# A layer kernel: x of most groups loaded already transposed and normalised by GpSimd, the k maxima folded into ScalarE's exp, and VectorE's steps on two PSUM banks merged

## The chip, the cores and the metric

The kernel runs on one core of a Trainium2 chip. The metric is device time in microseconds (us) of one execution. TensorE (PE), VectorE (DVE), ScalarE (ACT), GpSimd (POOL) and SyncE (SP, which only issues DMAs here) each work through a program of their own, in order, and meet at semaphores.

## The reference, cut to what matters

```
x: (128, 64, 256) f32;  8 heads of 32 channels;  cond: (128, 512)
xn = layernorm(x) * ln_w + ln_b
q  = softmax over the 32 channels of a head ( xn @ Wq + bq )
k  = softmax over the 64 tokens of a batch  ( xn @ Wk + bk + (1 - mask) * -1e6 )
v  = (xn @ Wv + bv) * mask
att = k^T v per batch and head;  y = q @ att
scale, shift = split( silu(cond) @ W_emb + b_emb )
h  = layernorm(y) * ln2_w + ln2_b;  h = h * (1 + scale) + shift
out = x + silu(h) @ W_out + b_out
```

## The kernel before

The 8192 rows of x are cut into 16 groups of 512 tokens (8 batches each, T = 4 tiles of 128 tokens). A group passes through three stages, and the order is written out by hand for each engine: in turn i, `body(i, ...)` does the front stage F of group i (transposed x, k, q, v), the middle stage B of group i-1 (attention and y) and the back stage O of group i-2 (second layer norm, silu, output product). Turns 3 to 14 are a loop of two turns, the others are unrolled, and a tail finishes the last groups. The helper `steps` calls `body`; N means that a next group exists.

**TensorE** in a turn: 8 transposes of the normalised x (L1059, into the banks bt), 8 transposes of exp(k) of the group before (L961), the k product (12 matmuls, `k_high` and `k_low`: every fp32 operand is split in a high and a low part, so each product is three), 8 transposes of y (L973), 8 of exp(q) (L982), 128 small attention matmuls, the q and v product of tiles 0 and 1, 128 small y matmuls, the q and v product of tiles 2 and 3, and the output product of the group two back (24 matmuls). All matmuls have the line of the helper, L905.

**ScalarE** copies the transposed x out of PSUM (this makes the high part xt_hi, L533), copies exp(k), exp(q) (L498, L515), does exp of k and q (L509, L505), tanh (L521, into the SBUF tile th), the v copies (L489), the high part of h (L526), the mask offset (L482), and normalises the four x tiles of the next group, row by row, with a scale and a bias per partition (L558).

**GpSimd** subtracts the k maxima from k (L356, two 128x512 steps), adds the shift to z (L271), takes the layer norm roots of x and of y (chains of four and of two tiny steps, each waiting for the one before, L402 to L408 and L420, L422), the low part of h (L367), normalises y (L425, four tiles) and adds b_out to x (`x_biased`, L375, one 128x1024 step).

**VectorE**: low part of x (L804, PSUM bank minus xt_hi, one step per bank), masked k and its maxima (L815, L819), z = y^T times the modulation (L735), statistics of x (L632, L636), the scaled attention kv (L747, L751), h = (tanh + 1) * z (L759, from th and z_s), q maxima and q minus them (L722, L727, one step per tile), y by its sums (L770, L775), statistics of y (L784 to L792) and the residual (L798, one step per bank).

**SyncE** loads x and the mask rows and stores the output; all transfers of a turn go through its one queue in the order of its program.

PSUM has 8 banks: be (two), bt (two) and the two pairs bk and bv. The four banks be and bt are also the tile by of the y product. A bank is written again only after its readers have counted up the semaphores that the writer waits for.

Of the kernel before, what the change touches and what calls it, by code (L numbers as in the profile page):

```python
# [20 lines left out]
def build_layer(nc, x, cond_t, columns_in, b_qvk, mask_rows, wq, wk, wv, w_emb, w_out, b_out, out):  # L21
# [23 lines left out]
    with ctx:  # L45
# [36 lines left out]
        xr = sb("xr", [P, 4, T])  # L82
        xhat = sb("xhat", [P, 2, T, D])
# [17 lines left out]
        th = sb("th", [P, C, GT])  # L101
        h_s = sb("h_s", [P, C, GT])
# [6 lines left out]
        h_t = xhat[:, 0, :, :].rearrange("p (c t) d -> p c (t d)", c=C)  # L109
# [12 lines left out]
        def bank(name):  # L122
            return ctx.enter_context(nc.psum_tensor(name, [P, 512], fp32))
# [3 lines left out]
        bk_ = [bank("bk0"), bank("bk1")]  # L127
        bv_ = [bank("bv0"), bank("bv1")]
# [14 lines left out]
        x_in = [sem("x_in0"), sem("x_in1")]  # L143
        x_first = [sem("x_first0"), sem("x_first1")]
# [80 lines left out]
        def steps(eng, body, tail, after_first=None):  # L225

            def at(i):
                body(i, i % 2, i + 1 < G, 0 <= i < G, 0 <= i - 1 < G, 0 <= i - 2 < G)
# [6 lines left out]
            with eng.Fori(1, G // 2 - 1) as turn:  # L235
                body(2 * turn + 1, 1, True, True, True, True)
                body(2 * turn + 2, 0, True, True, True, True)
            at(G - 1)
            tail()
# [4 lines left out]

        def first(i):

            return isinstance(i, int) and i == 0
# [25 lines left out]

        x_h = x.rearrange("(g t p) d -> g p t d", t=T, p=P)
# [12 lines left out]
        def _(sp):  # L287
# [15 lines left out]
            for n in range(2):  # L303
                sp.dma_start(w_e[n][:, :, :], w_emb[n * 2 * P:(n + 1) * 2 * P, :]
                             .rearrange("(c p) n -> p c n", p=P)).then_inc(we_in, 16)
            sp.dma_start(w_o, w_out.rearrange("(c p) n -> p c n", p=P)).then_inc(wo_in, 16)
            load_off(1, 1)
            sp.dma_start(bo_all[:, :], b_out[None, :].broadcast_to([P, D])).then_inc(bo_in, 16)

# [5 lines left out]
            def body(i, par, N, F, B, O):  # L315

                if N and not (isinstance(i, int) and i < 1):
                    wait(sp, xstat_d, 4 * i)
                    load_x(i + 1, 1 - par)
                    wait(sp, kadd_d, 2 * i)  # L320
                    load_off(i + 1, 1 - par)
                if O and not (isinstance(i, int) and i < 3):
                    store(i - 3)

# [18 lines left out]
        def _(pool):  # L343
# [6 lines left out]
            pool.memset(v_s[:, :, :, :, DH:AW], 1.0).then_inc(pool_init, 1)  # L350

            def k_shifted(g, parity, c):

                wait(pool, kmax_d, 2 * g + c + 1)
                kk = k_t[:, parity, c, :].rearrange("p (b s) -> p b s", s=SEQ)
# [13 lines left out]

            def x_biased(g):  # L370
                if isinstance(g, int) and g == 0:
                    pool.wait_ge(bo_in, 16)
                wait(pool, xhat_d, 4 * g + 4)
# [4 lines left out]
            def body(i, par, N, F, B, O):  # L378
                if F and not first(i):
                    k_shifted(i, par, 0)  # L380
                if O:
                    if isinstance(i, int) and i == 2:
                        pool.wait_ge(mod_ready, C)
                    shifts(i - 2)
                if last_turn(i):
                    k_shifted(i, par, 1)
                    x_biased(i)
                if N and isinstance(i, int) and i < 0:
                    pool.wait_ge(pool_init, 1)
                    pool.wait_ge(xmv_d, T)  # L390
                    nc.gpsimd.tensor_scalar(xr[:, 0, :], xmv[:, :, 1], 1.0, EPS, ALU.mult, ALU.add).then_inc(xr_d, 1)
                    pool.wait_ge(xr_d, 1)
                    nc.gpsimd.tensor_tensor(xr[:, 1, :], xr[:, 0, :], neg_half[:, :], ALU.pow).then_inc(xr_d, 1)
                    pool.wait_ge(xr_d, 4)
                    for t in (2, 3):
                        nc.gpsimd.tensor_scalar(xhat[:, 0, t, :], x_all[:, 0, t * D:t * D + D], xr[:, 1, t:t + 1],
                                                xr[:, 3, t:t + 1], ALU.mult, ALU.add).then_inc(xhat_d, 1)
                elif N:
                    g = i + 1
                    wait(pool, xhat_d, 4 * g)  # L400
                    wait_apart(pool, xmv_d, 4 * g + 4)
                    nc.gpsimd.tensor_scalar(xr[:, 0, :], xmv[:, :, 1], 1.0, EPS, ALU.mult, ALU.add).then_inc(xr_d, 1)  # L402
                    wait(pool, xr_d, 4 * g + 1)
                    nc.gpsimd.tensor_tensor(xr[:, 1, :], xr[:, 0, :], neg_half[:, :], ALU.pow).then_inc(xr_d, 1)
                    wait(pool, xr_d, 4 * g + 2)
                    nc.gpsimd.tensor_tensor(xr[:, 2, :], xmv[:, :, 0], xr[:, 1, :], ALU.mult).then_inc(xr_d, 1)
                    wait_apart(pool, xr_d, 4 * g + 3)
                    nc.gpsimd.tensor_scalar(xr[:, 3, :], xr[:, 2, :], -1.0, 1.0, ALU.mult, ALU.add).then_inc(xr_d, 1)  # L408
                if O:
                    for c in range(C):  # L410
                        h_low(i - 2, c)
                if first(i):
                    k_shifted(i, par, 0)
                if F and not last_turn(i):
                    k_shifted(i, par, 1)
                if B:
                    g = i - 1
                    wait(pool, yhat_d, 4 * g)
                    wait(pool, yve_d, 2 * g + 2)
                    nc.gpsimd.tensor_tensor(yr[:, 1, :], yr[:, 0, :], neg_half[:, :], ALU.pow).then_inc(yr_d, 1)  # L420
                    wait(pool, yr_d, 2 * g + 1)
                    nc.gpsimd.tensor_tensor(yr[:, 3, :], yr[:, 2, :], yr[:, 1, :], ALU.mult).then_inc(yr_d, 1)  # L422
                    wait_apart(pool, yr_d, 2 * g + 2)
# [3 lines left out]
                if F and not last_turn(i):  # L427
                    x_biased(i)

# [22 lines left out]
        def _(act):  # L452
# [19 lines left out]
            def emb_copied():  # L472

                act.wait_ge(emb_done, 1)
                for j in range(2 * C):
                    nc.scalar.activation(emb[:, j, :], be[1][:, j * BATCH:(j + 1) * BATCH], ACT.Identity,
                                         scale=0.5, bias=b_e[:, j:j + 1]).then_inc(emb_out, 1)

# [15 lines left out]
            def exp_k_copied(g):  # L494
                for e in range(2):
                    wait(act, ekt_d, 2 * g + e + 1)
# [673 lines left out]
```

## Time and profile before

| | us |
|---|---|
| median of 3 runs | 321.76 |
| lowest and highest run | 320.66, 323.11 |
| the profiled execution, whole | 320.57 |
| the profiled execution, span from first to last instruction | 318.8 |
| TensorE busy in the span | 305.2 |
| VectorE busy in the span | 276.6 |
| GpSimd busy in the span | 229.2 |
| ScalarE busy in the span | 192.7 |

The durations in the rows come from the profiled execution: 1.8 us of its time lie outside of the span, and the median of the runs is 1.2 us above it. Busy time counts the union of an engine's instructions. TensorE's instructions overlap, so a group's busy time divided by its count says what one costs the engine; the mean duration of one is longer.

### The profile page before, as it was taken

To read this page: it belongs to the slowest core of one execution; us is meant where nothing else is said; L and a number is where in the kernel's file an instruction comes from. 1 tells how busy PE (TensorE), PEld (TensorE's weight loads), DVE (VectorE), ACT (ScalarE), POOL (GpSimd) and SP (SyncE) were. 2 spreads that over 40 slices of the span, in tenths; PEclk is the share of its full clock that TensorE was granted. 3 is DMA by queue.
4 is the path that set the end of the run, shared out by engine and by line. 5 is a ranking of instruction groups with operands and counts; after the bars stand their busy time and mean duration, and the time that the engine had idled before them with its cause. 6 is when DMAs were issued, how large, how long until landed. Compare 5 with 4: busy or idle time off the path is not lost.

```text
span 318.8 us, 14540 instructions
## 1 busy us (share of the span) xinstructions
PE 305.2 (96%) x5650; PEld 261.3 (82%) x5650; DVE 276.6 (87%) x749; ACT 192.7 (60%) x378; POOL 229.2 (72%) x276
## 2 busy tenths in 40 slices
PE   6999989999999999999999999999999999998964
PEld 5587767889888898889888898889888898987854
DVE  3876989799898989899898989899898989889784
ACT  1556557656575757757575757657575748655350
POOL 2181479868777978878787888878787888886550
PEclk9999999999999999999999999999999999999978
DMA  6940301230504041130505041230505010100023
GB/s 218 348 117 1 103 3 37 64 105 4 167 3 148 16 132 33 62 102 0 164 0 153 11 132 33 67 98 0 164 0 153 11 66 0 67 4 4 2 69 132
DMA packets 21706, 23.84 MB, mean 75 GB/s; under 512 B 1073, under 2 KB 19121, under 8 KB 21682
## 3 DMA queue, kind: packets, MB, share of 16 engines
q1 hardware_dynamic: 20736, 22.94, 23.4%
q10 hardware_dynamic: 946, 0.57, 0.6%
q8 instruction: 17, 0.28, 0.4%
q14 instruction: 7, 0.06, 0.1%
HBM read 15.12 MB, written 8.39 MB: 74 GB/s over the span
## 4 chain that ended last, share of the span: by engine, by line
PE 81%; DVE 12%; issue 2%; DMA 2%; POOL 1%; ACT 1%; SPq 0%; DVEq 0%; POOLq 0%
PE bk L905 27%; PE bv L905 26%; PE by L905 13%; PE by L982 4%; PE bv L973 4%; PE by L961 4%; PE by L1059 4%; DMA q_t<-in_wv 2%; DVE ystat L784 1%; DVE h_s L759 1%; DVE y_s L775 1%; DVE xt_lo L804 1%; DVE xstat L632 1%; DVE q_s L727 1%; DVE qmax L722 1%
## 5 line engine op out<-in xcount | busy, mean ns | idle before, releaser
L509 ACT ACTIVATE k_t<-k_t 128x512 f32<-128x512 f32 x32 | 20.0, 626 | 42.9 <-POOL k_t L356 42.9
L356 POOL TENSOR_TENSOR k_t<-k_t,kmax 128x512 f32<-128x512 f32 x32 | 33.9, 1060 | 16.1 <-DVE kmax L819 16.1
L367 POOL TENSOR_TENSOR h_lo<-h_s,h_hi 128x512 fp32r<-128x512 f32 x30 | 39.1, 1325 | 2.5 <-ACT h_hi L526 1.9
L271 POOL TENSOR_TENSOR z_s<-z_s,mod_shift 128x512 f32<-128x512 f32 x30 | 30.7, 1045 | 14.2 <-DVE z_s L735 14.2
L375 POOL TENSOR_TENSOR x_all<-x_all,bo_all 128x1024 f32 (+1 forms) x16 | 38.9, 2433 | 0.0
L558 ACT ACTIVATE xhat<-x_all,xr 128x256 f32 (+1 forms) x62 | 32.2, 592 | 5.1 <-DVE xr L643 3.7
L425 POOL TENSOR_SCALAR y_s<-y_s,yr 128x256 f32<-128x256 f32 x60 | 32.8, 561 | 2.5 <-POOL yr L422 2.2
L815 DVE SCALAR_TENSOR_TENSOR k_t<-off,bk 128x512 f32<-128x512 f32 x32 | 21.8, 682 | 14.5 <-PE bk L905 14.5
L533 ACT ACTIVATE xt_hi<-by 128x512 fp32r<-128x512 f32 x32 | 17.4, 597 | 25.2 <-PE by L1059 25.2
L905 PE MATMUL bv<-w_o_hi,h_hi 128*128 128x256 f32 x120 | 32.2, 287 | 0.0
L905 PE MATMUL bv<-w_o_lo,h_hi 128*128 128x256 f32 x120 | 32.0, 288 | 0.0
L905 PEld LDWEIGHTS by<-kv,q_t 32*64 32x64 f32 x2048 | 22.4, 130 | 6.4 <-issue 5.3
L420 POOL TENSOR_TENSOR yr<-yr,neg_half 128x4 f32<-128x4 f32 x15 | 15.2, 1013 | 17.1 <-DVE yr L792 17.1
L905 PE MATMUL bk<-xt_hi,w_k_hi 128*128 128x512 f32 x64 | 26.6, 416 | 0.7 <-ACT xt_hi L533 0.7
L521 ACT ACTIVATE th<-z_s 128x512 f32<-128x512 f32 x30 | 18.9, 633 | 13.0 <-POOL z_s L271 13.0
L905 PE MATMUL bk<-xt_hi,w_k_lo 128*128 128x512 f32 x64 | 25.3, 395 | 0.0
L905 PE MATMUL by<-kv,q_t 32*64 32x33 f32 x2048 | 24.5, 226 | 0.4 <-issue 0.2
L905 PE MATMUL bv<-w_o_hi,h_lo 128*128 128x256 f32 x120 | 24.2, 283 | 0.0
L819 DVE TENSOR_REDUCE kmax<-k_t 128x8 f32<-128x512 f32 x32 | 22.0, 686 | 2.2
L905 PEld LDWEIGHTS bv<-w_o_hi,h_hi 128*128 128x128 f32 x120 | 23.2, 193 | 0.6
L905 PEld LDWEIGHTS bv<-w_o_lo,h_hi 128*128 128x128 f32 x120 | 23.1, 193 | 0.6
L804 DVE TENSOR_TENSOR xt_lo<-by,xt_hi 128x512 fp32r<-128x512 f32 x32 | 20.6, 685 | 3.2 <-ACT xt_hi L533 3.2
(128 smaller groups left out, 864.3 us busy)
## 6 DMA issues: line engine op xcount, KB each, us to landing
x_all<-in_x SPq DMA_DIRECT2D x15, 512.0 KB, 4.4
out<-x_all SPq DMA_DIRECT2D x15, 512.0 KB, 3.2
off<-in_mask_rows SPq DMA_DIRECT2D x16, 256.0 KB, 3.3
x_all<-in_x SPq DMA_DIRECT2D x2, 256.0 KB, 3.4
z_s<-in_w_emb SPq DMA_DIRECT2D x1, 512.0 KB, 9.2
h_s<-in_w_emb SPq DMA_DIRECT2D x1, 512.0 KB, 11.1
out<-x_all SPq DMA_DIRECT2D x2, 256.0 KB, 2.6
y_s<-in_wk ACTq DMA_DIRECT2D x1, 256.0 KB, 4.1
```

Of the source, the lines that this page charges most:

```text
L271: return eng.tensor_tensor(z, z, mod_shift[:, c, span(g, GB)].unsqueeze(2).broadcast_to([P, GB, SEQ]), ALU.add)
L356: nc.gpsimd.tensor_tensor(kk, kk, kmax[:, c, :].unsqueeze(2).broadcast_to([P, GB, SEQ]), ALU.subtract).then_inc(ksub_d, 1)
L367: nc.gpsimd.tensor_tensor(h_lo[:, c, :], h_s[:, c, :], h_hi[:, c, :].bitcast(fp32), ALU.subtract).then_inc(hlo_d, 1)
L375: nc.gpsimd.tensor_tensor(xg, xg, bo_all[:, :].unsqueeze(1).broadcast_to([P, T, D]), ALU.add).then_inc(xb_d, 1)
L425: nc.gpsimd.tensor_scalar(y_s[:, t, :], y_s[:, t, :], yr[:, 1, t:t + 1], yr[:, 3, t:t + 1], ALU.mult, ALU.add).then_inc(yhat_d, 1)
L509: nc.scalar.activation(k_t[:, parity, c, :], k_t[:, parity, c, :], ACT.Exp).then_inc(kexp_d, 1)
L521: nc.scalar.activation(th[:, c, :], z_s[:, c, :], ACT.Tanh, scale=0.5).then_inc(th_d, 1)
L558: nc.scalar.activation(xhat[:, 1 - par, t, :], group_of(x_all, g)[:, :, t * D:t * D + D].rearrange("p g n -> p (g n)"), ACT.Identity, scal ...
L804: nc.vector.tensor_tensor(xt_lo[:, c, :], bt[c][:, :], xt_hi[:, c, :].bitcast(fp32), ALU.subtract).then_inc(lo_d, 1)
L815: nc.vector.scalar_tensor_tensor(k_t[:, par, c, :], off[:, par, :], -1000000.0, bk_[c][:, :], ALU.mult, ALU.add).then_inc(kadd_d, 1)
L819: nc.vector.tensor_reduce(out=kmax[:, c, :], in_=k_t[:, par, c, :].rearrange("p (b s) -> p b s", s=SEQ), axis=AX.X, op=ALU.max).then_inc(k ...
L905: return nc.tensor.matmul(dst, lhsT, rhs, start=start, stop=stop)
```

## The change

The host gives a second input, x_t, which is x transposed. From group 2 on the transposes of x on TensorE are gone. Instead, SyncE loads the transposed raw x of the group (512 KB) into xt_raw. Its normalisation is now per column, so the layer norm's two numbers per token have to lie along the free axis, in every partition: GpSimd makes them per token as before (`x_rstd`), VectorE turns the 128x32 tile by blocks (`x_rows`), SyncE writes the rows to DRAM with four small DMAs (`rows_stored`) and reads them back broadcast to all partitions (`rows_loaded`, 4 KB per partition), and GpSimd multiplies and adds in place (`x_scaled`, two 128x512 steps per half of the channels). ScalarE makes the high part from xt_raw at the end of the turn before (`x_high`), VectorE the low part of both halves in one step (`x_low`).

From group 1 on `k_shifted` is gone. VectorE writes the negated masked k and takes its minimum; ScalarE's exp takes scale -1 and the minimum as bias. That works for one batch at a time, so the two exp steps of a group become sixteen steps of 128x64.

The four steps that normalise y move from GpSimd to ScalarE, at the start of the next turn (`y_hat_all`), except for the last groups. ScalarE's four steps on x are gone from group 2 on.

tanh is written to the PSUM banks bt instead of the SBUF tile th, once exp(q) is copied out of them. The y product waits for the h steps that read it there (wait on h_d).

VectorE's q maxima, q subtraction, k-v reciprocals, scaled y, low part of x and residual are done in one step for two banks each. x is loaded and its statistics are taken three groups ahead instead of one. The first turns and a few orders change with it.

The loop now covers turns 3 to 12. The core of the diff:

```diff
@@ SyncE
+            def load_xt(g, parity):
+                sp.dma_start(xt_raw[:, parity, :, :], xt_h[:, :, span(g, GT)]).then_inc(xt_in[parity], 16)
+            def rows_stored(g, parity):
+                wait(sp, xrow_d, g - 1)
+                wait(sp, rows_in, 16 * g - 48)
+                for n in range(4):
+                    sp.dma_start(rows_dram[parity].rearrange("k (t p) -> (k t) p", p=P)[:, 32 * n:32 * n + 32],
+                                 xr_rows[32 * n:32 * n + 2 * T, :]).then_inc(rows_out, 16)
+            def rows_loaded(g, parity):
+                wait(sp, rows_out, 64 * g - 64)
+                wait(sp, xs_d, 2 * g - 4)
+                sp.dma_start(rows[:, :, :].rearrange("p k n -> p (k n)").unsqueeze(1),
+                             rows_dram[parity:parity + 1].rearrange("o k n -> o (k n)").unsqueeze(0)
+                             .broadcast_to([P, 1, 2 * GT])).then_inc(rows_in, 16)
+            def body(i, par, N, F, B, O, S):
...
+                if S:
+                    wait(sp, xstat_d, 4 * i + 5)
+                    load_x(i + 3, 1 - par)
+                if N and not first(i):
                     wait(sp, kadd_d, 2 * i)
                     load_off(i + 1, 1 - par)
+                if not (isinstance(i, int) and i + 2 >= G):
+                    rows_stored(i + 2, par)
                 if O and not (isinstance(i, int) and i < 3):
                     store(i - 3)
+                if not (isinstance(i, int) and i + 2 >= G):
...
+                        load_xt(i + 2, par)
+                    rows_loaded(i + 2, par)
@@ GpSimd
-            def k_shifted(g, parity, c):
...
+            def x_scaled(g, parity, c):
+                if c == 0:
+                    wait(pool, rows_in, 16 * g - 16)
+                    wait(pool, xt_in[parity], 8 * (g - parity))
+                xc = xt_raw[:, parity, c, :]
+                nc.gpsimd.tensor_tensor(xc, xc, rows[:, 0, :], ALU.mult).then_inc(xm_d, 1)
+                wait(pool, xm_d, 2 * g + c - 3)
+                nc.gpsimd.tensor_tensor(xc, xc, rows[:, 1, :], ALU.add).then_inc(xs_d, 1)
...
+                for c in range(C):
+                    if N and c == 0 and not first(i):
+                        x_scaled(i + 1, 1 - par, c)
+                    if O:
                         h_low(i - 2, c)
+                    if N and c == 1 and not first(i):
+                        x_scaled(i + 1, 1 - par, c)
                 if B:
+                    y_scale(i - 1)
...
+                if S and not first(i):
+                    x_rstd(i + 3)
+                if not last_turn(i):
+                    x_biased(i)
@@ ScalarE
+            def x_high(g, parity, c):
+                wait(act, xs_d, 2 * g + c - 3)
+                wait(act, qv_d, 4 * g)
+                nc.scalar.activation(xt_hi[:, c, :], xt_raw[:, parity, c, :], ACT.Copy).then_inc(hi_d, 1)
             def k_exp(g, parity, c):
-                wait(act, ksub_d, 2 * g + c + 1)
-                nc.scalar.activation(k_t[:, parity, c, :], k_t[:, parity, c, :], ACT.Exp).then_inc(kexp_d, 1)
+                wait(act, kmax_d, 2 * g + c + 1)
+                for n in range(GB):
+                    kk = k_t[:, parity, c, n * SEQ:n * SEQ + SEQ]
+                    last = nc.scalar.activation(kk, kk, ACT.Exp, scale=-1.0, bias=kmax[:, c, n:n + 1])
+                last.then_inc(kexp_d, 1)
 (order of a turn: y_hat_all(i-2); exp_k_copied 0; q_exp(i-1, half 1); exp_k_copied 1; k_exp(i, 0);
  q_copied; z_tanh into bt; v_tile 0; h_high 0; v_tile 1; h_high 1; k_exp(i, 1); v_tile 2; v_tile 3;
  mask_offset; x_high(i+1, 0 and 1); q_exp(i, half 0))
@@ VectorE
+            def x_low(i, full):
+                wait(dve, hi_d, 2 * i + 2)
+                nc.vector.tensor_tensor(xt_lo[:, :, :], full, xt_hi[:, :, :].bitcast(fp32),
+                                        ALU.subtract).then_inc(lo_d, 2)
+            def x_rows(g):
+                wait(dve, xr_d, 4 * g + 4)
+                wait(dve, rows_out, 64 * g - 128)
+                nc.vector.transpose(xr_rows[:, :], xr[:, :, :].rearrange("p a t -> p (a t)")).then_inc(xrow_d, 1)
 (order of a turn: k_masked 0; k_max 0; k_masked 1; z_scaled(i-2); k_max 1; kv_scaled(i-1); h_product(i-2) 0, 1;
  x_stats(i+3); q_max 0; y_sums(i-1); q_shifted 0; y_scaled_all(i-1); y_stats(i-1); q_max 1; x_rows(i+2);
  q_shifted 1; x_low(i+1, xt_raw); residual_all(i-2))
@@ TensorE
-                if F:
-                    for c in range(C):
...
-                            last = nc.tensor.transpose(bt[c][:, t * P:t * P + P], xhat[:, par, t, c * P:c * P + P],
...
                 if B:
+                    wait(pe, h_d, 2 * i - 2)
                     y_product(i - 1)
```

## Rows read from the trace of the kernel before

**Rows 1.** The page: busy times, and the granted clock in 40 slices

```profile
PE 305.2 (96%) x5650; PEld 261.3 (82%) x5650; DVE 276.6 (87%) x749; ACT 192.7 (60%) x378; POOL 229.2 (72%) x276
...
PEclk9999999999999999999999999999999999999978
```

**Rows 2.** Windows: turns 3 to 14, then turn 15

```profile
60.92:275.53 214.61, 214.61 (x4179) 186.29 (x4178) 195.24 (x541) 140.43 (x277) 173.65 (x204) 1.00 0.23 70
275.53:290.95 15.42, 14.47 (x318) 11.72 (x317) 13.52 (x23) 9.19 (x18) 13.51 (x11) 1.00 0.11 37
```

**Rows 3.** Chain that ended last, k products of turns 9, 10

```profile
169.37 2.93 PE bk L905 x12
...
187.28 2.83 PE bk L905 x12
```

**Rows 4.** The same chain in turn 2 (start, us, what)

```profile
43.05 1.29 DVE xt_lo L804 x2
```

**Rows 5.** The same chain in turn 15 and the tail

```profile
285.04 2.85 DVE h_s L759
...
290.81 1.31 DVE ystat L784 x4
...
294.29 2.17 POOL y_s L425 x4
```

**Rows 6.** Groups of instructions by line, of all engines

```profile
L1059 PE MATMUL by<-ident,xhat 128*128 128x128 f32 x128 | 16.6, 273 | 0.0
...
L367 POOL TENSOR_TENSOR h_lo<-h_s,h_hi 128x512 fp32r<-128x512 f32 x30 | 39.1, 1325 | 2.5 <-ACT h_hi L526 1.9
L356 POOL TENSOR_TENSOR k_t<-k_t,kmax 128x512 f32<-128x512 f32 x32 | 33.9, 1060 | 16.1 <-DVE kmax L819 16.1
L425 POOL TENSOR_SCALAR y_s<-y_s,yr 128x256 f32<-128x256 f32 x60 | 32.8, 561 | 2.5 <-POOL yr L422 2.2
...
L422 POOL TENSOR_TENSOR yr<-yr 128x4 f32<-128x4 f32 x15 | 3.0, 200 | 1.2
...
L509 ACT ACTIVATE k_t<-k_t 128x512 f32<-128x512 f32 x32 | 20.0, 626 | 42.9 <-POOL k_t L356 42.9
...
L476 ACT ACTIVATE emb<-by,small 128x128 f32<-128x128 f32 x4 | 1.1, 369 | 0.2 <-PE by L905 0.2
...
L770 DVE RECIPROCAL rq<-by 128x32 f32<-128x32 f32 x16 | 5.5, 346 | 0.9 <-PE by L905 0.9
```

**Rows 7.** Timeline of turn 9, TensorE

```profile
167.46 1.04 PE L1059 MATMUL by<-ident,xhat 128*128 128x128 f32 x8
...
168.33 1.04 PE L961 MATMUL by<-ident,k_t 128*128 128x128 f32 x8
```

**Rows 8.** Timeline of turn 9, VectorE

```profile
171.11 0.69 DVE L815 SCALAR_TENSOR_TENSOR k_t<-off,bk 128x512 f32<-128x512 f32 x1 [1.00 <-PE bk L905]
...
173.83 1.28 DVE L735 TENSOR_TENSOR z_s<-bv,mod_scale 128x512 f32<-128x512 f32 x2
...
177.58 1.28 DVE L759 SCALAR_TENSOR_TENSOR h_s<-th,z_s 128x512 f32<-128x512 f32 x2
178.78 0.75 DVE L722 TENSOR_REDUCE qmax<-bv 128x8 f32<-128x256 f32 x2
```

**Rows 9.** Timeline of turn 9, GpSimd

```profile
177.16 1.02 POOL L404 TENSOR_TENSOR xr<-xr,neg_half 128x4 f32<-128x4 f32 x1
178.25 0.67 POOL L406 TENSOR_TENSOR xr<-xmv,xr 128x4 f32<-128x4 f32 x1
```

**Rows 10.** Timeline of turn 15, VectorE, then GpSimd

```profile
283.78 4.12 DVE L759 SCALAR_TENSOR_TENSOR h_s<-th,z_s 128x512 f32<-128x512 f32 x2
...
284.53 2.82 POOL L375 TENSOR_TENSOR x_all<-x_all,bo_all 128x1024 f32<-128x1024 f32 x1
```

**Rows 11.** The page: DMA queues and issues

```profile
q1 hardware_dynamic: 20736, 22.94, 23.4%
...
x_all<-in_x SPq DMA_DIRECT2D x15, 512.0 KB, 4.4
```

More of the change, by code:

```diff
@@ L233, in steps @@
                 at(i)
[L235 to L238, printed above, removed]
+            with eng.Fori(1, G // 2 - 2) as turn:
+                body(2 * turn + 1, 1, True, True, True, True, True)
+                body(2 * turn + 2, 0, True, True, True, True, True)
+            for i in (G - 3, G - 2, G - 1):
+                at(i)
             tail()
@@ L272, in shift, with first @@
                                      ALU.add)
+        def first(i):
+            return isinstance(i, int) and i == 0
+        xt_h = x_t.rearrange("(c p) n -> p c n", p=P)
         x_h = x.rearrange("(g t p) d -> g p t d", t=T, p=P)
@@ L384, in body @@
                     shifts(i - 2)
+                if first(i):
+                    k_shifted(0)
+                    k_shifted(1)
+                    x_rstd(2)
                 if last_turn(i):
-                    k_shifted(i, par, 1)
                     x_biased(i)
[L388 to L408, printed above, removed]
@@ new lines, in x_high_turned, with x_hat_one @@
+            def x_high_turned(g):
+                for c in range(C):
+                    act.wait_ge(xt_d, 2 * g + c + 1)
+                    wait(act, qv_d, 4 * g)
+                    nc.scalar.activation(xt_hi[:, c, :], bt[c][:, :], ACT.Copy).then_inc(hi_d, 1)
+            def x_hat_one():
+                act.wait_ge(xr_d, 8)
+                act.wait_ge(xt_d, 2)
+                for t in range(T):
+                    nc.scalar.activation(xhat[:, t, :], x_all[:, 1, t * D:t * D + D], ACT.Identity,
+                                         scale=xr[:, 0, t:t + 1], bias=xr[:, 1, t:t + 1]).then_inc(xhat_d, 1)
@@ new lines, in emb_copied, with k_exp_first, exp_k_copied @@
+            def emb_copied():
+                act.wait_ge(emb_done, 1)
+                for j in range(2 * C):
+                    nc.scalar.activation(emb[:, j, :], be[1][:, j * BATCH:(j + 1) * BATCH], ACT.Identity,
+                                         scale=0.5, bias=b_e[:, j:j + 1]).then_inc(emb_out, 1)
+            def k_exp_first(c):
+                act.wait_ge(ksub_d, c + 1)
+                nc.scalar.activation(k_t[:, 0, c, :], k_t[:, 0, c, :], ACT.Exp).then_inc(kexp_d, 1)
+            def exp_k_copied(g, e):
+                wait(act, ekt_d, 2 * g + e + 1)
+                wait(act, att_d, g)
+                nc.scalar.activation(e_k[:, 2 * e:2 * e + 2, :].rearrange("p t d -> p (t d)"), be[e][:, :],
+                                     ACT.Copy).then_inc(ek_d, 1)
@@ new lines, in body @@
+                v_tile(i, par, 1)
+                if O:
+                    h_high(i - 2, 1)
+                if first(i):
+                    x_hat_one()
+                else:
+                    k_exp(i, par, 1)
+                v_tile(i, par, 2)
+                if first(i):
+                    k_exp_first(1)
+                    emb_copied()
+                v_tile(i, par, 3)
+                if N:
+                    mask_offset(i + 1, 1 - par)
+                    if first(i):
+                        x_high_turned(1)
+                    else:
+                        for c in range(C):
+                            x_high(i + 1, 1 - par, c)
@@ L1033, in out_product, with x_transposed @@
                           ).then_inc(o_d, 1)
+            def x_transposed(g):
+                pe.wait_ge(xhat_d, 4 * g + 4)
+                for c in range(C):
+                    for t in range(T):
+                        last = nc.tensor.transpose(bt[c][:, t * P:t * P + P], xhat[:, t, c * P:c * P + P], ident[:, :])
+                    last.then_inc(xt_d, 1)
             def k_high(i, c):
```

373 lines of the change are left out of this document (203 added, 170 removed).

## The prediction

> **What bounds the kernel now.** The page comes first: TensorE is busy for 305 of 318.8 us at a granted clock of 9 tenths or more until the very end, so the clock plays no part, and VectorE follows with 87% [rows 1]. A share over the span hides where each engine is full, so the windows come next. Turns 3 to 14 take 214.61 us, 17.88 each, and TensorE is busy in all of it; per turn VectorE works 16.27 us, GpSimd 14.47 and ScalarE 11.70 [rows 2]. In these turns the path is TensorE's own list of work. The chain of waits says the same: its k product takes 2.93 and 2.83 us in two turns following one another [rows 3], so there is a stall of 0.1 us for the low part of x in one of two turns, and nothing more. Outside of the loop it is otherwise. In turn 2 the chain runs through VectorE and reaches the k product through the low part of x [rows 4]. In turn 15 TensorE is busy for 14.47 of 15.42 us [rows 2], and the chain runs through an h step of 2.85 us on VectorE and four y steps on GpSimd [rows 5].
>
> **The change on TensorE.** It loses eight transposes of x per group. They start at 167.46, the next eight at 168.33 [rows 7]: 0.87 us on the path, not the 1.04 that the row shows as busy nor 8 times 273 ns. The group row gives the same order, 16.6 us for 128, 1.04 per eight, the overlap with the neighbour included [rows 6]. With the 0.05 us of mean stall a turn's floor is 17.88 - 0.87 - 0.05 = 16.96 us. For turns 3 to 14 that would be 12 x 0.92 = 11.0 us. Whether it is reached depends on whether the others fit in 17 us and keep their order.
>
> **VectorE**, per turn. Merged steps save an instruction's fixed part: the pair of 128x256 steps takes 0.75 us, one step of 128x512 takes 0.69 [rows 8], so a merge is worth 0.06. The q maxima and the q subtraction are two merges each, the reciprocals, scaled y, low part of x and residual one each: 8 x 0.06 = 0.5 us. `x_rows` adds a 128x32 step: its nearest rows are the 0.35 us of another 128x32 step [rows 6] and nothing at all; I take 0.2. Sum: 16.27 - 0.5 + 0.2 = 16.0 us (15.8 to 16.1). It fits into 17, with the 1.00 us in which it waits for k now [rows 8], a wait that stays, since the residual and the first k bank hang on two moments of TensorE's turn 2.5 us apart.
>
> **ScalarE.** Four x steps leave and four y steps of the same kind come: nothing. Two exp steps of 0.63 [rows 6] become sixteen of 128x64 with a bias per partition. No row shows that shape. The nearest is the emb copy, 128x128 with such a bias: 4 in 1.1 us of which the last takes 0.37, so 0.25 from start to start [rows 6]. Half the columns can't cost more; from below I take 0.2. Sum: 11.70 - 1.25 + 16 x 0.24 = 14.3 us (13.7 to 14.6), well below 17. The Trainium skill (ScalarE: Activation LUTs, What ACT_TABLE_LOAD costs) gives an ACTIVATE with a pointer bias as 280 ns plus 0.833 ns per column and an overlap of 93 ns back to back; an estimate from it is 240 ns for 64 columns. By it the sum would be the same; for the shape with 128 columns it gives 387 ns where the row has 369, so trace and page agree.
>
> **GpSimd** loses k minus maxima (2 x 1.06) and the four y steps (32.8 us for 60, so 2.19 [rows 6]), and gets four steps of 128x512 on two full operands. Nearest rows: 1.06 us with a broadcast operand, 1.325 for h_lo with two full ones [rows 6]. `rows` is a full operand, so I take 1.25. Sum: 14.47 - 2.12 - 2.19 + 5.0 = 15.2 us (14.4 to 15.5), to which waits between dependent steps add some 0.3. It fits, but the order matters, so I lay out a turn, each step with the time it has in turn 9 now and the new ones with the prices above. Zero is the start of the transposes of exp(k) (168.33 in turn 9); TensorE's work follows in its old order.
>
> - k masked at 2.7 as before (171.11 is 2.78 [rows 8]); z now ahead of the second maximum, at 4.8 instead of 5.5 (173.83 [rows 8]).
> - GpSimd: shifts 5.5 to 7.6, first x half to 10.2, low parts of h to 12.8, second x half to 15.3, y root to 16.8, x root to 18.9, `x_biased` to 21.3. That is 4.3 in the next turn, where the shifts are due at 5.5. TensorE needs the low parts of h at about 14.5: 1.7 to spare.
> - ScalarE: exp of k until 6.2, q copied 7.2, tanh to 8.3, x high at 15.4 and 16.0 after mask offset, half of exp(q) to 17.1, y steps to 2.3 in the next turn; TensorE transposes y at 3.7.
> - VectorE: h until 9.1, statistics of x to 10.8, y statistics to 15.3, `x_rows` at 16.0, x low 16.7 to 17.9, residual to 19.0, which is 2.0 of the next turn, ahead of k at 2.7. The low part is needed at 1.8 and is there at 0.9.
> - New wait on TensorE: the y product waits for h, since tanh lies in its banks. It is due at 9.6, h is done at 9.1: 0.5 to spare. Behind it in the queue stand two q and v tiles and the output product, and everything waits.
>
> Every margin is positive, the thinnest are 0.5 and 1.2 us. I take a turn of 17.05 us, 0.09 above the floor, for small waits like those of now. Turns 3 to 14: 12 x 0.83 = 10.0 us.
>
> **The new transfers.** `x_rows` at 16.0, four small DMAs issued one by one in 1.6 us, landing, then the broadcast read of 512 KB, issued behind a store and the load of the transposed x. A load of 512 KB takes 4.4 us from issue to landing [rows 11]; the packets of q1 take 23.4% of 16 engines for 22.94 MB, so 512 KB occupy them for 1.7 us. Written at 17.6, landed at about 19.8, read issued at 20.1, landed between 23.5 (nothing ahead) and 26.0 (two transfers of 1.7 us ahead, less what has passed of them). In the next turn this is 6.5 to 9.0. GpSimd wants it at 7.6 and can take it until 9.4 before the low parts of h come late to the output product. So it costs nothing in this sum, by up to 2 us of cover. Traffic rises by about 1 MB a turn, to 40% of the engines.
>
> **Start.** The first turns exchange work: statistics of x come earlier, `weights_o` moves from turn 1 to turn 0, where VectorE waited for v. VectorE's low part of x for group 2 ends at 44.33 now [rows 4]; adding the merged and moved steps I find the same within 0.5 us. From there TensorE has no x transposes at the head of turn 3: 0.9 saved (0 to 1.5).
>
> **Turn 15.** Now the two h steps of this turn take 4.12 us instead of 1.28, while GpSimd runs its 128x1024 step, which takes 2.82 [rows 10]. Both inputs of h, th and z_s, lie in SBUF. In the changed kernel tanh lies in PSUM. The small steps show the other side of it: in turn 9 a 128x4 step takes 0.67 us with the h steps at work (177.58 to 178.86), while its kind takes 0.20 [rows 6, 8, 9]. So the collision goes. The 2.85 us step is on the chain, which goes on through the y statistics to the four y steps of GpSimd [rows 5]; without the wait it takes the 0.68 of its kind, 2.17 less. Not all of that comes back, since y also waits for TensorE's y product. In my layout the statistics of y begin at 13.6 in the turn; now they begin at 290.81 - 275.53 = 15.3 [rows 2, 5]. That is 1.7 us, and with a little lost in the tail I take 1.6 for turn 15 and tail together (0.8 to 2.2).
>
> **Sum.** 0.9 + 10.0 + 1.6 = 12.5 us. The profiled execution took 320.57 in all, so 308.1; the median lies 1.2 above it, so 309.3. I say 309.
>
> **Rivals.**
> Small waits each turn, at 20%: exp pieces at 0.3 us would put tanh and h 0.5 us later and use up the margin before the y product; GpSimd's steps at the upper end do the same to the low parts of h. Against it: every row is below that. At 17.4 us a turn: 12 x 0.48 + 2.5 = 8.3, 313.5 us.
>
> No gain, at 11%: the rows come late. Each us beyond 9.4 holds GpSimd, and behind it in its queue the low parts of h and TensorE's output product. The path from one `x_rows` through the output product spans two turns, so half of it counts per turn. To cancel the 0.83 us of a turn it takes a landing 1.7 us beyond 9.4, 12 us after `x_rows`. Then only start and end remain: 319.3 us. For it speaks that four transfers, a store and a load share one queue; against it the 4.4 us of a load as it is.
>
> Slower, at 11%: the two-input steps move to a worse place. `x_low` takes xt_raw and xt_hi, both in SBUF, where it took a PSUM bank before. It runs near the end of the turn, where GpSimd soon starts its 2.4 us `x_biased`. In my layout it starts at 16.7 and GpSimd's step at 18.9, and only tiny steps meet it. If x high comes over 2.2 us late, `x_low` meets `x_biased` and waits as h did in turn 15, 2.85 - 0.68 = 2.17 us, with TensorE's k product behind it: 17.05 + 2.17 = 19.22 us a turn, 12 x 1.34 - 2.5 = 13.6 us slower, 335 us. The Trainium skill (SBUF — State Buffer, SBUF: two separate sides) states that a VectorE operation with two SBUF inputs and a GpSimd operation exclude each other for a whole instruction, whichever starts first; the 4.12 us pair agrees. By that rule the change also gives relief in each turn, since h leaves it and `x_low` enters.
>
> **Chances and range.** The forecast has 58%, the three rivals 20, 11 and 11. The lower end is the floor, 16.96 a turn, with the best start and end: 11.0 + 1.5 + 2.2 = 14.7, or 307, less the 1.2 us by which runs differ: 305.5. The upper end takes in small waits and stops short of no gain: 318. A difference within 1% is about what this kernel's runs can't tell from none. Faster by over 1%: the forecast and the first rival, 0.78; within: 0.11; slower: 0.11.
>
> **What would show it.** Turn length from one L961 group to the next at 17.0 to 17.1; no idle time of TensorE before the y product put down to h, none before k put down to x_lo; exp pieces 0.2 to 0.26 us apart; GpSimd's x steps at 1.25; the broadcast read landed before the shifts of z end; h pair at 1.3 in turn 15. Wrong it would be if GpSimd stood waiting for the rows for over 2 us a turn, if its x steps took over 1.6, or if `x_low` showed durations over 2 us.

## The result and the profile after

The changed kernel takes 342.34 us in the median of 4 runs (335.77 to 344.56), the kernel before 321.95 (320.66 to 323.11). The ratio is 1.050, with an interval of 1.043 to 1.058: the change makes the kernel 5% slower, where 309 us was forecast. Medians and ranges take in all executions; the ratios, here and below, leave out those that fell in a slower state of the chip. The profiled execution took 335.77 us, with a span of 333.9.

The page of the changed kernel, busy times and granted clock, to be held against [rows 1]:

```profile
PE 302.2 (90%) x5538; PEld 253.7 (76%) x5538; DVE 274.2 (82%) x639; ACT 236.1 (71%) x588; POOL 245.0 (73%) x247
...
PEclk9799978999979999999999999999999999999789
```

TensorE is idle for 31.7 us of the span, against 13.6 before, and its clock, which was at its upper level nearly throughout, has dips. The windows of turns 3 to 14, of turn 15, of the tail, and of two short stretches in turns 2 and 4 (columns: PE, PEld, DVE, ACT, POOL busy, clock, DMA share, GB/s; [rows 2] has the same of before):

```profile
67.97:289.33 221.36, 208.92 (x4083) 176.90 (x4081) 189.09 (x439) 175.37 (x444) 187.52 (x175) 0.99 0.40 124
289.33:303.38 14.05, 14.05 (x319) 11.79 (x317) 11.79 (x20) 11.96 (x32) 10.50 (x7) 1.00 0.12 40
303.38:333.90 30.52, 21.74 (x385) 20.31 (x383) 19.60 (x48) 10.37 (x18) 11.09 (x15) 0.87 0.16 53
48.00:54.00 6.00, 4.89 (x15) 3.89 (x16) 3.60 (x7) 4.04 (x9) 5.59 (x7) 0.58 0.46 141
91.30:98.60 7.30, 5.21 (x78) 3.95 (x76) 4.13 (x14) 2.73 (x6) 4.45 (x5) 0.77 0.53 166
```

Turns 3 to 14 take 18.45 us each, TensorE works 17.41 of them, and no engine is full: VectorE works 15.76 us a turn, GpSimd 15.63, ScalarE 14.61. The forecast had 16.0, 15.2 (to 15.5) and 14.3, so the work was sized nearly right. What was added is waiting. Against the forecast of 60.0, 204.6 and 43.3 - 1.6 = 41.7 us for the three stretches, the start takes 68.0 us (8 over), turns 3 to 14 take 221.4 (17 over), turn 15 and the tail 44.6 (3 over).

The chain of waits names the way in the middle of the kernel. Around turn 8 it leaves TensorE altogether (start, us, what):

```profile
146.27 6.45 DMA x_all<-in_x
152.94 0.44 DVE xstat L741
...
160.16 0.21 DVE xr_rows L751
160.49 0.30 SPq L315
...
162.11 0.42 SPq L348
162.79 0.40 SPq L308
163.43 0.69 SPq L322
164.42 6.71 DMA x_all<-in_x
171.37 0.44 DVE xstat L741
```

This is a ring. The statistics of x begin at 152.94. VectorE reaches `x_rows` 7.2 us later. SyncE's queue has waited for it: four row writes (L315), a store (L348), the transposed x (L308), the read of the rows (L322), and only behind them the load of x, at 164.42, 4.3 us after `x_rows`. It lands 6.7 us later, and the next statistics, which have waited for it, begin at 171.37. Once round is 18.4 us, the length of this turn (18.46). The waits (us in total, times, longest) show VectorE waiting for x, GpSimd waiting for the rows themselves, and where the delay reaches TensorE: the k product waits until the late q subtraction has read its bank.

```profile
POOL xt_raw L424 <- DMA rows<-rows_dram: 15.6, 12, 2.6
...
DVE xstat L741 <- DMA x_all<-in_x: 11.7, 9, 1.7
...
PE bk L1058 <- DVE q_s L845: 9.3, 10, 1.7
```

A load of 512 KB of x takes 6.4 us to land now, against 4.4 [rows 11]; the broadcast read of the rows takes 5.8. From the page:

```profile
x_all<-in_x SPq DMA_DIRECT2D x15, 512.0 KB, 6.4
...
rows<-rows_dram SPq DMA_DIRECT2D x14, 512.0 KB, 5.8
```

The start has another cause. VectorE's modulation in turn 1, five steps of 0.28 to 0.35 us in the kernel before, from the timeline of after:

```profile
36.19 0.99 DVE L818 TENSOR_SCALAR emb<-emb 128x256 f32<-128x256 f32 x1
37.22 1.26 DVE L820 TENSOR_SCALAR mod_scale<-emb,small 128x128 f32<-128x128 f32 x1
38.40 1.37 DVE L822 SCALAR_TENSOR_TENSOR mod_shift<-emb,small 128x128 f32<-128x128 f32 x1
39.70 1.37 DVE L820 TENSOR_SCALAR mod_scale<-emb,small 128x128 f32<-128x128 f32 x1
40.99 0.34 DVE L822 SCALAR_TENSOR_TENSOR mod_shift<-emb,small 128x128 f32<-128x128 f32 x1
```

Three of the five are as long as one of GpSimd's steps on x, the first takes 0.99, and the last, when GpSimd is done, its normal 0.34. GpSimd's four steps on x run in just this time:

```profile
35.73 1.30 POOL L424 TENSOR_TENSOR xt_raw<-xt_raw,rows 128x512 f32<-128x512 f32 x1 [1.20 <-DMA rows<-rows_dram]
37.11 1.29 POOL L426 TENSOR_TENSOR xt_raw<-xt_raw,rows 128x512 f32<-128x512 f32 x1
38.36 1.26 POOL L424 TENSOR_TENSOR xt_raw<-xt_raw,rows 128x512 f32<-128x512 f32 x1
39.70 1.28 POOL L426 TENSOR_TENSOR xt_raw<-xt_raw,rows 128x512 f32<-128x512 f32 x1
```

The modulation takes from 36.19 to 41.33, 5.1 us instead of 1.3. TensorE idles behind it, and its k product of turn 2 takes 4.82 us, in the stretch whose mean granted clock is 0.58; the k product of turn 1 takes 3.26 in the same profile (29.81 to 33.08). And in turn 4 the chain has a gap that no engine explains:

```profile
90.45 0.89 PE by L1058 x56
91.34 2.09 issue
93.42 0.55 PE by L1058 x30
93.97 4.53 PE bv L1058 x12
```

TensorE waits 2.1 us for nothing that the profile shows, in the middle of its attention matmuls, and then does in 4.53 us what takes 2.99 at full clock; the mean granted clock of the stretch is 0.77.

### The profile page after: what moved, and what is told of

Its sections match the earlier page's. It is cut to its first block, busy times and chain, and to the rows that moved or that the text cites. A ratio compares the mean times of both kernels' runs of the same rounds, so it can differ in the third digit from the quotient of the medians.

```text
span 333.9 us, 14365 instructions
## 1 busy us (share of the span) xinstructions
PE 302.2 (90%) x5538; PEld 253.7 (76%) x5538; DVE 274.2 (82%) x639; ACT 236.1 (71%) x588; POOL 245.0 (73%) x247
## 4 chain that ended last, share of the span: by engine, by line
PE 35%; DVE 20%; DMA 18%; issue 13%; SPq 8%; ACT 2%; POOL 2%; DVEq 1%; POOLq 1%
DMA x_all<-in_x 15%; PE bv L1058 12%; PE bk L1058 11%; PE by L1058 6%; DVE y_s L918 4%; SPq L315 3%; DVE ystat L933 3%; DVE xstat L741 3%; DVE q_s L845 2%; PE by L1135 2%; DMA q_t<-in_wv 2%; SPq L322 2%; PE bv L1126 2%; DVE ymv L936 1%; DVE rq L913 1%
## 5 line engine op out<-in xcount | busy, mean ns | idle before, releaser
L615 ACT ACTIVATE k_t<-k_t,kmax 128x64 f32<-128x64 f32 x240 | 60.5, 336 | 6.2 <-DVE kmax L863 6.1
L424 POOL TENSOR_TENSOR xt_raw<-xt_raw,rows 128x512 f32<-128x512 f32 x28 | 36.2, 1293 | 15.6 <-DMA rows<-rows_dram 15.6
L455 POOL TENSOR_TENSOR x_all<-x_all,bo_all 128x1024 f32 (+1 forms) x16 | 40.1, 2508 | 0.2
L426 POOL TENSOR_TENSOR xt_raw<-xt_raw,rows 128x512 f32<-128x512 f32 x28 | 36.1, 1288 | 2.2
L569 ACT ACTIVATE y_s<-y_s,yr 128x256 f32<-128x256 f32 x56 | 29.1, 590 | 10.8 <-POOL yr L447 10.8
L1058 PE MATMUL bk<-xt_hi,w_k_hi 128*128 128x512 f32 x64 | 27.7, 433 | 9.6 <-DVE q_s L845 9.3
L741 DVE BATCH_NORM_STATS2 xstat<-x_all 128x6 f32 (+1 forms) x64 | 22.4, 413 | 11.7 <-DMA x_all<-in_x 11.7
L1058 PE MATMUL bv<-w_o_lo,h_hi 128*128 128x256 f32 x120 | 31.7, 285 | 0.0
L554 ACT ACTIVATE v_s<-bk,small 128x256 f32<-128x256 f32 x32 | 15.2, 476 | 20.5 <-PE bk L1058 19.3
L433 POOL TENSOR_SCALAR xr<-xmv 128x4 f32<-128x4 f32 x15 | 14.9, 993 | 15.8 <-DVE xmv L745 12.3
L1058 PEld LDWEIGHTS bv<-w_o_hi,h_hi 128*128 128x128 f32 x120 | 23.3, 194 | 3.7 <-DVE q_s L845 3.3
L1058 PE MATMUL by<-v_s,e_k 64*32 64x33 f32 x2048 | 21.1, 201 | 4.7 <-issue 3.0
L1058 PEld LDWEIGHTS by<-v_s,e_k 64*32 64x32 f32 x2048 | 19.1, 105 | 7.7 <-issue 5.7
L554 ACT ACTIVATE v_s<-bv,small 128x256 f32<-128x256 f32 x32 | 15.1, 475 | 13.5 <-PE bv L1058 13.5
```

Of the source, the lines that this page charges most:

```text
L424: nc.gpsimd.tensor_tensor(xc, xc, rows[:, 0, :], ALU.mult).then_inc(xm_d, 1)
L426: nc.gpsimd.tensor_tensor(xc, xc, rows[:, 1, :], ALU.add).then_inc(xs_d, 1)
L433: nc.gpsimd.tensor_scalar(xr[:, 2, :], xmv[:, :, 1], 1.0, EPS, ALU.mult, ALU.add).then_inc(xr_d, 1)
L455: nc.gpsimd.tensor_tensor(xg, xg, bo_all[:, :].unsqueeze(1).broadcast_to([P, T, D]), ALU.add).then_inc(xb_d, 1)
L554: nc.scalar.activation(v_s[:, par, t, :, 0:DH], bqv[t][:, D:2 * D].rearrange("p (h d) -> p h d", d=DH), ACT.Copy, scale=mask_c[:, i * T + ...
L569: nc.scalar.activation(y_s[:, t, :], y_s[:, t, :], ACT.Identity, scale=yr[:, 1, t:t + 1], bias=yr[:, 3, t:t + 1]).then_inc(yhat_d, 1)
```

## The experiments

**Load of x a turn earlier.** x_all has room for all groups, so the load can leave before the row writes.

```diff
-                if S:
-                    wait(sp, xstat_d, 4 * i + 5)
-                    load_x(i + 3, 1 - par)
+                if first(i):
+                    wait(sp, xstat_d, 5)
+                    load_x(3, 1)
...
+                if not (isinstance(i, int) and i + 4 >= G):
+                    wait(sp, xstat_d, 4 * i + 12)
+                    load_x(i + 4, par)
                 if not (isinstance(i, int) and i + 2 >= G):
                     rows_stored(i + 2, par)
```

> Changed kernel with the load of x issued one turn earlier, ahead of the four row writes; nothing else moves. Theory A (the ring x statistics, row writes, SyncE's queue, load of x, x statistics sets the turn): VectorE no longer waits for x (11.7 us in the changed kernel), the turn falls from 18.45 to 17.0 to 17.4 us, 12 turns give back 12 to 17 us, and the time comes to 322 to 328. Theory B (the rows themselves come late and hold GpSimd): GpSimd's wait for the rows grows to over 2 us a turn, and the turn stays above 18.

Measured: 334.98 us (331.32 to 336.68), ratio 1.047 (1.035 to 1.059). VectorE's wait for x is gone, GpSimd's for the rows stays at 11.4 us. Ten turns of it, and then turns 13 and 14:

```profile
64.25:240.66 176.41, 172.30 (x3403) 146.69 (x3402) 162.42 (x380) 145.47 (x370) 156.55 (x149) 1.00 0.42 129
240.66:284.50 43.84, 38.03 (x682) 32.31 (x681) 29.88 (x61) 29.34 (x76) 31.41 (x29) 0.88 0.34 98
```

The ten take 17.64 us each, where the same ten take 18.27 in the changed kernel (67.97 to 250.71). So the load of x was one of two limits, and without it the rows hold the turn. Neither theory had it alone: A's 17.0 was not reached, B's wait of over 2 us neither. The expected 322 to 328 us were missed mainly for another reason, turns 13 and 14, which take 23.3 and 20.6 us. Their chain:

```profile
247.43 3.79 issue
251.22 0.32 PE by L1061 x4
251.54 5.27 PE bv L1061 x12
...
282.88 1.05 ACT xt_hi L566 x2
...
284.02 2.85 DVE xt_lo L873
```

Again the gap in the issue, 3.8 us this time, and the slow clock behind it. At 284.02 stands the collision that the prediction described for `x_low`: 2.85 us for a step of 1.22, while `x_biased` runs on GpSimd (283.38, 2.40 us), once.

**Rows earlier.** One small step moves up, from behind the second q maximum to behind kv.

```diff
                 if B:
                     kv_scaled(i - 1)
+                if not first(i) and not (isinstance(i, int) and i + 2 >= G):
+                    x_rows(i + 2)
...
                 q_max(i, 1)
-                if not (isinstance(i, int) and i + 2 >= G):
+                if first(i):
                     x_rows(i + 2)
```

> Changed kernel with only VectorE's small turning step of the rows moved forward by about 7 us in its turn, behind the kv step. The row writes leave earlier, and the queue of SyncE behind them with it. Theory A and B both expect a gain here: the load of x lands some 5 us earlier and the rows 3 to 5 us earlier, turn 17.0 to 17.3 us, time 320 to 326. If the turn is set by neither (contention of GpSimd and VectorE for SBUF), it stays at 18 or more.

Measured: 316.29 us (315.01 to 316.75), ratio 0.988 (0.985 to 0.991). This one move puts the changed kernel ahead of the kernel before. The profiled executions differ by 20.8 us (335.77 and 315.01), the medians by 26. The turn came as expected; the time expected with it, 320 to 326 us, was put too high.

```profile
66.01:271.40 205.39, 203.15 (x4083) 176.10 (x4082) 188.24 (x440) 174.74 (x444) 187.45 (x176) 1.00 0.42 130
```

Turns 3 to 14 take 205.39 us, forecast were 204.6. Ten of the twelve take 16.85 to 16.90 us each, turns 4 and 13 take 18.1 and 18.5. GpSimd waits for rows once, 1.0 us; VectorE for x never. The bytes of a turn are the same, yet a load of x now lands after 5.3 us and the read of the rows after 4.3, where the changed kernel had 6.4 and 5.8.

**Both moves.**

> Both moves together. By A and B nothing is left to gain over the better of the two: within 1 us a turn is at 17.0 to 17.3, time 320 to 326; what remains over the forecast of 309 is then the start, about 7 us late against the kernel before, and the tail, 2.7.

Measured: 315.04 us (310.96 to 317.86), ratio 0.979 (0.961 to 0.997), turns 3 to 14 in 205.54 us. With the rows early the load of x is early enough too, as expected; the time is below the expected 320 to 326 again.

**No round trip.** SyncE's `rows_stored` and `rows_loaded` return at once for all groups but group 2, and GpSimd waits for the first rows only.

> Changed kernel whose row writes and the broadcast read are done for group 2 alone; the other groups are multiplied with group 2's rows, so the normalisation of x is left out for them. It shows the changed kernel without the round trip. A: turn 17.0 to 17.2, no wait for x, time 318 to 324. If the extra 128x512 steps of GpSimd or the exp pieces of ScalarE set the turn, it stays at 18.

Measured: 319.9 us (318.9 to 327.0), ratio 0.995 (0.989 to 1.001). Nine of the twelve turns take 16.86 to 16.90 us, so neither GpSimd's added steps nor ScalarE's pieces hold the turn. `x_rows` runs 16.4 us after the head of turn 9, where the changed kernel has it 19.4 us after the head of turn 7. Turns 3, 4 and 13 take 18.3, 18.4 and 19.8, with issue gaps of 0.7 to 1.8 us in them. The loads of x and x_t are no longer spaced by the waits for the rows; whether that moves the gaps was not tried. The early turns stay late as in the changed kernel.

**Modulation moved.** With the rows early, besides: the five steps go to the end of turn 0, before GpSimd has x to work on.

```diff
                     x_low(1, by[:, 2:4, :])
+                    modulation()
                     x_stats(3, 1)
...
-                if isinstance(i, int) and i == 1:
-                    modulation()
```

> The run with the rows' turning step early, and besides that the modulation's five steps moved from turn 1 to the end of turn 0, where GpSimd has no 128x512 step in flight. Theory C (in turn 1 these steps, three of which run in VectorE's fast mode or read two SBUF operands, wait for GpSimd's steps on x, 5.1 us for 1.3, TensorE then idles and goes on at half clock): turn 1 loses 3 to 4 us, the k product of turn 2 goes back from 5.5 to 2.8 us, and the time comes to 308 to 312. Rival: the start is set by the longer chain of x (transfers, GpSimd, low part), then under 2 us come back.

Measured: 312.71 us (308.7 to 316.9), ratio 0.955 (0.943 to 0.968). Turn 1 takes 15.2 us (18.1 with the rows early alone), turn 2 takes 19.2 (22.2), and the twelve matmuls of its k product 3.26 (from 49.50), where the rows early alone have 5.49 (from 47.08). Theory C's 3 to 4 us of turn 1 are 2.9. The windows of turns 3 to 14 and of turn 15 and the tail:

```profile
65.79:270.10 204.31, 203.16 (x4082) 176.18 (x4081) 188.27 (x440) 174.67 (x444) 187.42 (x176) 1.00 0.42 132
270.10:284.15 14.05, 14.05 (x318) 11.79 (x317) 11.79 (x20) 11.96 (x32) 10.50 (x7) 1.00 0.12 40
284.15:312.00 27.85, 18.83 (x385) 17.49 (x383) 19.43 (x48) 10.27 (x18) 11.09 (x15) 0.98 0.18 59
```

> The same with the load of x a turn earlier as well. Theory A says nothing more to gain once the rows go early: within 1 us of the run without it, 308 to 312. If the load of x still cost something, 1 to 3 us less.

Measured: 310.75 us (309.5 to 313.9), ratio 0.960 (0.950 to 0.970), the same as without the earlier load of x within the spread. These two are the fastest kernels of the study. The early turns don't repeat, though: turns 1 and 2 take 18.2 and 18.8 us here, since TensorE has a gap of 1.5 us in its issue in turn 1 and does the twelve matmuls behind it in 4.56 us.

**Modulation alone.** The changed kernel with only that second move.

> Changed kernel with only the modulation's steps moved to the end of turn 0; the rows leave as late as in the changed kernel. Theory C: turn 1 and the k product of turn 2 give back 5 to 6 us together, turns 3 to 14 stay near 18.4, time 334 to 338. If the early turns were late because of the rows' transfers, nothing comes back.

Measured: 339.39 us (329.6 to 341.3); no ratio can be given. In its profiled execution the five steps are back at 0.28 to 0.35 us each (33.39 to 34.72) and turn 1 takes 15.1 us, 3.1 less than in the changed kernel. Turn 2 takes 21.8, only 0.4 less: its k product still takes 4.61 us (from 48.48), although TensorE idled for the same 1.88 us ahead of it as in the run with the rows early and the modulation moved, where it takes 3.26. So the modulation is what lengthens turn 1, and its part in the slow k product of turn 2 is not shown; of the 5 to 6 us that theory C expected, 3.5 come back. Turns 3 to 12 take 18.37 us each, as in the changed kernel (18.27), turns 13 and 14 take 24.0 and 20.6. The time as a whole says nothing clear.

**Traffic alone.** The kernel before, with two further loads of 512 KB each turn.

```diff
                     load_off(i + 1, 1 - par)
+                    wait(sp, sp_in, 32 * i - 32)
+                    for n in range(2):
+                        sp.dma_start(spare[:, n, :].rearrange("p (t d) -> p t d", t=T), x_h[n]).then_inc(sp_in, 16)
```

> Kernel before with two further loads of 512 KB in each turn from the second on, into a tile that nothing reads: the traffic of the changed kernel without its work. Theory D (transfers in flight delay TensorE's instruction supply in the turns in which new code is reached, 4 and 13, and the clock falls after the gap): idle time put down to issue grows from 0.3 us to 1 to 4 us in one or two turns, the kernel loses 1 to 5 us. Rival: traffic alone costs nothing, time 321 to 323.

Measured: 330.16 us (326.9 to 332.0), ratio 1.015 (1.001 to 1.028). Turns 3 and 4 take 19.2 and 22.0 us instead of 18.1 and 17.8, turns 5 to 14 take 17.8 to 17.9 as before. The chain in turn 4:

```profile
94.81 0.66 PE by L915 x45
95.47 2.38 issue
97.85 1.04 PE by L915 x64
98.89 4.54 PE bk L915 x12
```

No engine has more work here. The gap, and the slow clock behind it, appear with the traffic. The profiled execution is 10.5 us longer than before, twice what was expected at most: 5.3 us in turns 3 and 4, 1.6 in turns 1 and 2, 3.3 in the stretch up to turn 1.

**tanh in PSUM alone**, on the kernel before, with the wait of the y product for h.

```diff
-                    wait(act, h_d, 2 * g)
-                    nc.scalar.activation(th[:, c, :], z_s[:, c, :], ACT.Tanh, scale=0.5).then_inc(th_d, 1)
+                    wait(act, qt_d, 2 * g + c + 3)
+                    nc.scalar.activation(home[c], z_s[:, c, :], ACT.Tanh, scale=0.5).then_inc(th_d, 1)
...
+                    wait(pe, h_d, 2 * i - 2)
                     y_product(i - 1)
```

> Kernel before with only tanh written to the PSUM banks. By the prediction the two h steps of turn 15 take 1.3 instead of 4.1 us, turn 15 and the tail lose 0.8 to 2.2 us, turns 3 to 14 stay at 17.88 since TensorE sets them: 319.6 to 321. Rival: the y statistics wait for the y product anyway, under 0.5 us.

Measured: 330.08 us (328.9 to 332.1), ratio 1.022 (1.011 to 1.033): slower, where no theory had it slower. Turn 15 does fall, from 15.42 to 14.11 us, but each turn before it grows from 17.88 to 18.63. The waits of this run name the step:

```profile
PE by L906 <- DVE h_s L760: 8.8, 13, 0.8
```

In the old order h ends after the y product is due, so the wait that the prediction called 0.5 us early is 0.75 late there. In the changed kernel z stands ahead of the second k maximum and h ahead of the statistics of x, and the wait costs next to nothing.

**tanh in SBUF**, the reverse, on the kernel with both moves of small steps.

> The run with rows early and modulation moved, with tanh back in its SBUF tile and without the wait of the y product for h. Theory E (two SBUF inputs of a VectorE step and a GpSimd step exclude each other): now the h steps meet GpSimd's 128x512 steps on x, which begin right behind the shifts; h steps of 1.3 us become 2 to 3.5 us and GpSimd's x steps wait too, turn 17.2 to 18.2 us, time 315 to 328. Rival: the wait taken away is worth more than the collision, turn stays at 16.9, time 308 to 313.

Measured: 330.14 us (328.4 to 337.0), ratio 1.019 (1.009 to 1.030). Turns 3 to 14 take 18.62 us each instead of 17.03, more than was expected. VectorE, then GpSimd, in turn 9:

```profile
164.81 3.29 DVE L902 SCALAR_TENSOR_TENSOR h_s<-th,z_s 128x512 f32<-128x512 f32 x2
```

```profile
164.58 1.29 POOL L424 TENSOR_TENSOR xt_raw<-xt_raw,rows 128x512 f32<-128x512 f32 x1
165.95 1.60 POOL L426 TENSOR_TENSOR xt_raw<-xt_raw,rows 128x512 f32<-128x512 f32 x1
167.52 3.00 POOL L415 TENSOR_TENSOR h_lo<-h_s,h_hi 128x512 fp32r<-128x512 f32 x2
```

The h pair takes 3.29 us instead of 1.28, and GpSimd's pair of low parts of h, 2.54 in the run with tanh in PSUM, takes 3.00. tanh in PSUM is worth 1.6 us a turn in this kernel and costs 0.75 in the other: its value comes from the other parts of the change.

## Why the prediction was wrong

**TensorE's floor was right.** 16.96 us a turn was forecast; where nothing waits it is 16.88, in ten turns of the run with the rows early. With both small steps moved, turns 3 to 14 take 204.3 us against 204.6 forecast, turn 15 and tail 41.9 against 41.7, and the time is 311 to 313 us against 309. That the twelve turns add up to the forecast is in part luck: eleven of them take 16.84 to 17.00 us, below the 17.05 of the forecast, and turn 13, at 18.44 with its issue gaps, makes up for it. The start is 5.8 us over its forecast even there (65.8 for 60.0). The sum described a kernel that differs from the changed one in the place of two small groups of VectorE steps.

**The step that failed is the one called "the new transfers"**, which were to cost nothing "by up to 2 us of cover". It followed the rows from `x_rows` to GpSimd, and there its bounds held, counted from `x_rows`: 7.5 to 10 us were allowed, and in turn 8 `x_rows` at 160.16 is answered by GpSimd's step at 169.28, 9.1 us. But it looked at the turn once, from a zero at which everything was on time, and never closed the path. Its `x_rows` stood at 16.0 in the turn, and it runs at 16.4 where the round trip is taken out; in the changed kernel it runs at 19.4, and all that was counted from it is late with it. It left out what else stands in SyncE's queue behind the row writes: the load of x three groups ahead, for which VectorE waits ahead of `x_rows`. That load was in the diff, and the prediction didn't give it a landing time. With the 4.4 us of [rows 11] the ring is 7.2 + 4.3 + 4.4 + 0.2 = 16.1 us and is hidden, with 0.9 us of margin under 17. At the 6.7 us that the load takes in it, it is 18.4. So besides the missing term a landing time was too small: the prediction took that of the kernel before for a kernel with 60% more bytes. The bytes alone don't set it, as the 5.3 us with the rows early show. And the delay was looked for at the output product, by way of the low parts of h; TensorE shows it at the k product (9.3 us in ten waits, against 1.0 in two for the low parts of h).

**The rival with this mechanism, rows late, had 11%** and was priced as no gain, 319 us. Its mechanism is one half of what was found, without the load of x; its price doesn't hold. Taking the load of x out gives 0.63 us a turn back (turns 3 to 12, 18.27 to 17.64); with the rows early the same turns take 17.00, 0.64 less again. In the profiled executions the 15.2 us lost against the kernel before are 7.1 in the start, 6.8 in turns 3 to 14 (18.45 for 17.88) and 1.3 in turn 15 and the tail; the rival priced the turns at no loss and kept the gains at start and end.

**The start** was to gain 0.9 us and lost 7 against the kernel before. The prediction's word for it was that it finds "the same within 0.5 us" after adding steps. It did name the collision of a VectorE step with two SBUF inputs, for h and for `x_low`, but not for the modulation, although GpSimd's steps on x were new in just that turn. Of the 7 us, turn 1 accounts for 2.9, turn 2 for 2.6 and the stretch up to turn 1 for 1.5. Moving the modulation brings turns 1 and 2 from 40.3 to 34.4 us in one pair of profiles, 0.5 better than the 34.9 of before; in the two other pairs it brings them from 38.7 to 37.0 and from 40.4 to 36.9. The stretch up to turn 1 takes from 25.4 to 31.4 us in the profiles of all kernels here, with a slow or a fast clock in it, and 29.3 in the kernel before with added traffic. What decides it was not tried.

**Turn 15 and the tail.** Turn 15 falls to 14.05 us and the tail stays at 27.7 to 28.1 in the runs with the rows early or without the round trip, with 27.85 in the run with both small steps moved, 1.4 us less in sum than before, forecast 1.6. In the changed kernel itself the tail takes 30.5 at a mean clock of 0.87; why the clock is lower there was not followed.

**The other terms.** ScalarE's exp pieces: eight take 2.02 us, 0.24 from start to start, as estimated. GpSimd's steps on x: 1.29, taken 1.25. The row step: 0.20, taken 0.2. VectorE's sum: 15.8, forecast 16.0. The rival of small waits didn't come by way of the y product in the changed kernel. The lower end of the range comes out at 305.9 by its own terms, not 305.5, which changes nothing. The slower rival, `x_low` against the 128x1024 step, occurs once, in the run with x early. Otherwise the small steps of GpSimd pay: its first step of the x root takes 0.99 us in the mean instead of 0.20, behind `x_low`, and there is room for that.

## What to carry to other kernels

Close each new path through a queue into a ring and add it up once round: from the step that frees or writes, through everything issued in order in front of the transfer, to the step that waits, and back. Its margin is the turn minus that sum, and the turn is the new, shorter one. List for each queue what stands behind a new wait, and give every one of these transfers a landing time with the other traffic in flight, not that of the quiet kernel.

A helper's step has a place besides a length: the same five small steps cost 1.3 us or 5.1, and the row step costs about 21 us of the whole or nothing, by where they stand in the order.

## What the runs showed of the hardware

- VectorE's steps of one SBUF tensor and a scalar, TENSOR_SCALAR on 128x128, take 0.28 us alone and 1.26 to 1.37 while GpSimd works on 128x512 (turn 1 of the changed kernel). The Trainium skill (SBUF — State Buffer, Who interferes with whom) gives the exclusion for VectorE's two-port modes as well as for two SBUF inputs; the 5.1 us of the five steps agree with it.
- TensorE's issue stops, for 0.4 to 3.8 us at a time, in turns 1 to 4, 13 and 14 of the changed kernel and its variants, and in no run by over 0.3 us ahead of a matmul in turns 5 to 12; in the tail there are some of up to 1.1. Turns 1 and 2 are unrolled, turns 3 and 4 are the first pass through the loop's two bodies, and turns 13 and 14 stand behind the loop: in all of them the instructions run for the first time. That it is the supply of instructions is an inference from those places.
- The kernel before has no such gap; with 1 MB of loads more per turn it has four, 1.0 to 2.4 us, in turns 1 to 4. So traffic favours them. But it neither makes them alone nor always: the kernel before with only tanh moved has one of 1.4 us in turn 2, and the run with tanh back in SBUF, with all the traffic, has none up to turn 15.
- Behind such gaps, and behind idle time of TensorE in turn 2, twelve matmuls of 2.8 to 3.3 us take 4.5 to 5.5 in several runs. In the 5.6 us of the k product in turn 2 of the run with the rows early the granted clock is 0.50, the lower level of 1.2 GHz. It doesn't follow each time: after the same 1.88 us of idle time the k product of turn 2 takes 3.26 us in one run and 4.61 in another.
